# A two-layer tower on one Trainium2 core: the first layer's experts multiplied in split float32r instead of float32

## The reference, cut to what matters

```python
def _L0_ffn_ref(x, gate_w, w_gate, w_up, w_down, sh_gate, sh_up, sh_down, se_gate_w):   # 8 experts, hidden 256
    scores = xf @ gate_w.T
    ew, ei = jax.lax.top_k(scores, TOP_K)                       # 2 of 8 for each token
    ew = jax.nn.softmax(ew, axis=-1)
    x1 = jax.nn.silu(jnp.einsum('td,ehd->teh', xf, w_gate))
    x3 = jnp.einsum('td,ehd->teh', xf, w_up)
    expert_out = jnp.einsum('teh,edh->ted', x1 * x3, w_down)
    ...
    shared = jax.nn.silu(xf @ sh_gate.T) * (xf @ sh_up.T) @ sh_down.T      # hidden 512
    sgate = jax.nn.sigmoid(xf @ se_gate_w.T)
    return (routed + sgate * shared).reshape(Bb, Tt, Cc)
```

## Time and profile before

| | |
|---|---|
| median of 3 runs | 1573.73 us (1570.84 to 1576.62) |
| the profiled execution's own time | 1577.39 us |
| its span, first to last instruction | 1575.6 us |
| mean granted TensorE clock | 0.968 of full speed |
| busy: TensorE, VectorE, ScalarE, GpSimd | 1390.4, 838.1, 373.3, 480.1 us |
| moved by DMA | 197.16 MB, 125 GB/s over the span |

### The profile page before, as it was taken

How to read it: one execution, slowest core, us unless ns; L and a number is a source line. 1 busy time by engine, 2 the same in 40 slices (tenths; PEclk the granted TensorE clock), 3 DMA queues, 4 the chain that set the end, 5 groups by cost and what they waited for, 6 DMA issues and landing times.

```text
span 1575.6 us, 21975 instructions
## 1 busy us (share of the span) xinstructions
PE 1390.4 (88%) x6461; PEld 1080.0 (69%) x6462; DVE 838.1 (53%) x1729; ACT 373.3 (24%) x711; POOL 480.1 (30%) x350
## 2 busy tenths in 40 slices
PE   0595648999999999379999889999999999999997
PEld 0583316888544444237777578888888889999896
DVE  8875597755322222563667775555555543333332
ACT  1113113111111111242222312232333212222221
POOL 0661430252244443100111015632332203343332
PEclk9999779999999999798999999999999999999999
DMA  4493005201865554700000403656666579776443
GB/s 97 89 161 39 0 21 179 104 21 63 304 149 93 87 89 72 204 22 0 1 0 1 182 21 97 206 199 212 208 221 225 189 267 361 243 198 185 78 73 41
DMA packets 88931, 197.16 MB, mean 125 GB/s; under 512 B 28657, under 2 KB 32753, under 8 KB 85361
## 3 DMA queue, kind: packets, MB, share of 16 engines
q1 hardware_dynamic: 68768, 154.33, 30.1%
q0 software_dynamic: 20096, 42.02, 14.6%
HBM read 112.24 MB, written 81.02 MB: 123 GB/s over the span
## 4 chain that ended last, share of the span: by engine, by line
PE 79%; DVE 13%; issue 3%; DMA 2%; ACT 1%; POOLq 1%; POOL 0%; SPq 0%; DVEq 0%; ACTq 0%
PE ps L1533 25%; PE ps L1593 19%; PE ps L1655 9%; PE ps L2055 6%; PE ps L1681 4%; PE ps L429 4%; PE ps L1623 2%; DVE held L482 2%; PE ps L538 2%; PE ps L1669 1%; PE ps L778 1%; PE ps L2080 1%; PE ps L779 1%; PE ps L2027 1%; PE ps L2111 1%
## 5 line engine op out<-in xcount | busy, mean ns | idle before, releaser
L1593 PE MATMUL ps<-moe_rounded 128*128 128x384 f32 (+2 forms) x1800 | 374.7, 350 | 0.0
L1593 PEld LDWEIGHTS ps<-moe_rounded 128*128 128x128 f32 x1800 | 326.3, 188 | 33.3
L1300 DVE SCALAR_TENSOR_TENSOR held<-ps,moe_scratch,held 128x512 f32<-128x512 f32 (+1 forms) x255 | 187.5, 747 | 180.8 <-PE ps L1533 180.0
L1533 PE MATMUL ps<-moe_expert_parts,moe_rows_parts 128*128 (+1 forms) x1320 | 258.4, 349 | 2.5 <-DVE moe_rows_parts L1324 1.5
L1533 PE MATMUL ps<-moe_rounded 128*128 128x512 f32 (+3 forms) x885 | 242.2, 394 | 11.8 <-DVE moe_rounded L1282 9.7
L1533 PEld LDWEIGHTS ps<-moe_expert_parts,moe_rows_parts 128*128 128x128 f32 (+1 forms) x1320 | 219.6, 190 | 15.8 <-issue 3.3
L1533 PEld LDWEIGHTS ps<-moe_rounded 128*128 128x128 f32 (+2 forms) x885 | 146.7, 171 | 50.7 <-DVE moe_rounded L1282 12.0
L1310 DVE TENSOR_TENSOR moe_scratch<-moe_scratch,ps 128x256 f32<-128x256 f32 (+1 forms) x80 | 37.7, 471 | 237.2 <-ACT moe_scratch L1515 237.2
L1655 PE MATMUL ps<-moe_experts,moe_scratch 128*128 x320 | 144.2, 593 | 0.6 <-issue 0.6
L1404 POOL TENSOR_TENSOR moe_split_parts<-moe_scratch,moe_split_parts 128x704 fp32r<-128x704 f32 (+2 forms) x48 | 88.6, 1851 | 172.9 <-ACT moe_split_parts L1497 172.9
L1388 POOL DMA_INDIRECT slot_tokens<-moe_scratch x68 | 73.5, 1081 | 174.2 <-DVE held L1300 167.4
(11 more groups left out here) (311 smaller groups left out, 1686.2 us busy)
## 6 DMA issues: line engine op xcount, KB each, us to landing
moe_expert_parts<-expert_parts SPq DMA_DIRECT2D x8, 3840.0 KB, 13.0
expert_parts<-moe_split_parts SPq DMA_DIRECT2D x32, 704.0 KB
moe_scratch<-in_ffn_gate_up SPq DMA_DIRECT2D x32, 352.0 KB, 4.7
xn_rows<-moe_xn SPq DMA_DIRECT2D x2, 4096.0 KB, 12.9
moe_experts<-in_ffn_gate_up SPq DMA_DIRECT2D x8, 1024.0 KB, 6.3
expert_parts<-moe_split_parts SPq DMA_DIRECT2D x8, 1024.0 KB
moe_scratch<-in_ffn_sh_gate_up SPq DMA_DIRECT2D x15, 512.0 KB, 3.5
tokens<-sb SPq DMA_DIRECT2D x16, 256.0 KB
```

The lines of the kernel that those rows point to most:

```text
L1300: v.scalar_tensor_tensor(out=hb[0:rows, t, :], in0=ps[0:rows, ADDED[t % 3], :], scalar=sg[0:rows, t:t + 1], in1=hb[0:rows, t, :], op0=ALU. ...
L1533: mm = t.matmul(out, lhs(k, x), rhs(k, y), start=(k == 0 and i == 0), stop=(k == ks - 1 and i == 2))
L1593: mm = t.matmul(unit_banks(u, m)[j], weights(k, x, j), xT[y][:, k, unit_cols(m)], start=(k == 0 and i == 0), stop=(k == KD - 1 and i == 2))
```

## The change

Layer 0's experts now work as layer 1's: weights in two rounded parts, a ring of four slots, three matmuls for each product, hi and lo parts of the turned rows and hidden rows, and `tile_slots` in the routing. Their weights come as 48 pieces of 128x512 (six for each of the eight experts: four of gate and up, two of down), through a ring of four small slots: SP loads a piece (256 KB), ScalarE rounds it (`round`), GpSimd subtracts (`rest`), SP stores both parts (512 KB) in DRAM. Pieces 0 to 23 are made in the scan layer: four loads are put into the tokenizer's SP program, 4 roundings stand ahead of the scan layer's ScalarE program and 20 after its sigmoids; GpSimd's first four stand ahead of its additions of beta and 20 behind them. Pieces 24 to 47 are made in layer 0's shared blocks 0 to 2, eight in each. All four shared blocks of layer 0 are now written out without a loop.

The core of the diff:

```diff
+EARLY_SLOTS, EARLY_W, EARLY_CHUNKS = 4, D, KD + 2
+EARLY, EARLY_FIRST, EARLY_FRONT, EARLY_BLOCKS = NE * EARLY_CHUNKS, 4, 24, 3
+EARLY_EACH = (EARLY - EARLY_FRONT) // EARLY_BLOCKS
+class EarlyParts:
...
+    def keep(self, sp, n):
...
+        sp.wait_ge(self.lo, n + 1)
+        sp.dma_start(to, self.part(n).bitcast(F32)).then_inc(self.stored[n % EARLY_SLOTS], 16)
+    def keep_front(self, sp):
+        for n in range(EARLY_FRONT):
+            self.keep(sp, n)
+            if n + EARLY_SLOTS < EARLY_FRONT + 2:
+                self.load(sp, n + EARLY_SLOTS)
+    def round(self, s, n):
+        x, turns = n % EARLY_SLOTS, n // EARLY_SLOTS
+        s.wait_ge(self.loaded[x], 16 * (turns + 1))
+        if turns:
+            s.wait_ge(self.stored[x], 16 * turns)
+        s.activation(self.part(n)[:, 0], self.raw(n), ACT.Copy).then_inc(self.hi, 1)
+    def rest(self, p, n):
+        p.wait_ge(self.hi, n + 1)
+        p.tensor_tensor(self.part(n)[:, 1], self.raw(n), self.part(n)[:, 0], ALU.subtract).then_inc(self.lo, 1)
...
@@ sync of a mixture, layer 0
-            for e in range(2):
-                load_expert(sp, e, e_in[0])
-            more(2)
-            with sp.Fori(3, NSH) as b:
-                more(b)
+            for n in range(EARLY_FRONT + 2, EARLY_FRONT + EARLY_SLOTS):
+                early_parts.load(sp, n)
+            for b in range(EARLY_BLOCKS):
+                early_parts.keep_beside(sp, b)
+                if b + 2 < NSH:
+                    more(b + 2)
+            early_parts.all_kept(sp)
             slots_in()
-            sp.wait_ge(e_in[0], 2 * 16 * WD)
-            sp.sem_inc(rt, 1)
+        load_parts(sp, 0)
+        sp.wait_ge(e_in[0], E0 + LOADED)
+        sp.sem_inc(rt, 1)
...
@@ ScalarE, the "part" steps of a shared block
+                    if not by_block:
+                        if b < EARLY_BLOCKS:
+                            n = EARLY_FRONT + b * EARLY_EACH
+                            for k in EARLY_AT[m]:
+                                early_parts.round(s, n + k)
...
@@ GpSimd, layer 0
             for n in range(2 * T):
                 beside_adds(n)
+                for k in rest[:n % 2]:
+                    early_parts.rest(p, k)
+                rest = rest[n % 2:]
...
@@ TensorE, gate and up of a tile
-            elif 2 * F <= QC:
-                for k in range(KD):
-                    mm = t.matmul(ps[:, u, 0:2 * F], xgT[:, u, k], exg(e, k, 0, 2 * F), start=(k == 0), stop=(k == KD - 1))
+            if 2 * F <= QC:
+                mm = split_products(ps[:, u, 0:2 * F], lambda k, x: xgT[:, u, x, k],
+                                    lambda k, y: slots_w[:, slot, y * GW + k * KW:y * GW + (k + 1) * KW], KD)
...
-        ROUTING = {("lo", 0): segments, ("lo", 1): slots_of, ("lo", 2): tile_slots if split_w else tile_experts}
+        ROUTING = {("lo", 0): segments, ("lo", 1): slots_of, ("lo", 2): tile_slots}
...
+EARLY_AT = ((0, 1), (2,), (3, 4), (5,), (6,), (7,))
```

More of the change, by code:

```diff
@@ L696, in gpsimd @@
     def gpsimd(p):
+        for n in range(EARLY_FIRST):
+            early_parts.rest(p, n)
         p.wait_ge(w_fb, 16 * 7)
@@ L702, in gpsimd @@
             p.tensor_tensor(hb[0:r, n, :], hb[0:r, n, :], bet[0:r], ALU.add).then_inc(hbr, 1)
+        for n in range(EARLY_FIRST, EARLY_FRONT):
+            early_parts.rest(p, n)
         p.wait_ge(hbr, T)
@@ L709, in scalar @@
     def scalar(s):
+        for n in range(EARLY_FIRST):
+            early_parts.round(s, n)
         for k, tiles in enumerate(GROUPS):
@@ L819, in ffn_layer @@
     GW, DW = KD * 2 * F, NF * D
-    EW = 2 * (GW + DW) if split_w else GW + DW
+    EW = 2 * (GW + DW)
     SGW = KD * 2 * SF
-    if not split_w:
-        ex = g.experts[:, 0:NE * EW].rearrange("p (e w) -> p e w", e=NE)
-    exg, exd = (lambda e, k, j, w: ex[:, e, k * 2 * F + j:k * 2 * F + j + w]), (lambda e, f, r: ex[0:r, e, GW + f * D:GW + (f + 1) * D])
+    by_block = early_parts is None
     r = Arena(g.rounded, g.y_at, g.y_at)
@@ L1063, in blocks @@
     def blocks(eng, body):
-        first = FIRST if split_w else 1
+        first = FIRST if by_block else NSH - 1
         pairs = (NSH - 1 - first) // 2
@@ L1068, in blocks @@
             body(b, b % 2)
-        with eng.Fori(0, pairs) as i:
-            for k in range(2):
-                body(2 * i + first + k, (first + k) % 2)
+        if pairs:
+            with eng.Fori(0, pairs) as i:
+                for k in range(2):
+                    body(2 * i + first + k, (first + k) % 2)
         for b in range(2 * pairs + first, NSH):
@@ L1273, in block @@
             for what, m in DVE_STEPS:
-                if split_w and is_last(b) and (what, m) == ("lo", NU - 1):
+                if is_last(b) and (what, m) == ("lo", NU - 1):
                     rows_lo(0, 0)
@@ L1380, in gpsimd @@
     def gpsimd(p):
+        if not by_block:
+            for n in range(EARLY_FRONT, EARLY_FRONT + EARLY_EACH):
+                early_parts.rest(p, n)
         p.wait_ge(rt, ROUTED)
@@ L1408, in gpsimd @@
         else:
+            rest = list(range(EARLY_FRONT + EARLY_EACH, EARLY))
             for n in range(2 * T):
                 beside_adds(n)
+                for k in rest[:n % 2]:
+                    early_parts.rest(p, k)
+                rest = rest[n % 2:]
+            assert not rest
         p.wait_ge(xs, 4 * 16)
@@ L2187, in look_through @@
         self.rounded = over("moe_rounded", self.y_at, self.high_at, F32R)
-        self.experts = over("moe_experts", self.xn_at, self.xn_at + EXPERTS)
         self.expert_parts = over("moe_expert_parts", self.xn_at, self.xn_at + PARTS, F32R)
```

245 lines of the change are left out of this document (130 added, 115 removed).

## The result

The changed kernel took 1599.37 us in the median of 4 runs (1598.41 to 1600.32), the one before 1575.15 us beside it (4 runs). The ratio is 1.0158, 95% interval 1.0143 to 1.0173: 24 us slower, where 16 faster was forecast. The span of the profiled execution is 1596.6 us, against 1575.6.

What follows compares the result with a forecast made beforehand. TensorE was taken as the bound, except VectorE in block 0. The terms -28.2 + 4.8 + 5.8 + 0.7 + 0.5 = -16.4 took the profiled 1577.4 to 1561.0, or 1557 us against the runs' median; range 1545 to 1569.

Steps and rivals of the forecast that it cites:

- The expert tiles: Layer 0's expert stage: tiles fall to 4.90 us, products of 512 columns at 0.230 or 0.241; 207.0 against 235.2, -28.2 us.
- 11.0 around the tiles: Layer 1's expert stage time beyond its forty tiles, 11.0 us, charged to layer 0's new stage in place of its 2.8.
- the chain of rows: Expert tile: rows turned, copied by ScalarE, rests by VectorE; 1.95 us within 2.06, hidden. Rival if not: 1573 us, chance 0.14.
- The scan layer: Pieces made in GpSimd's and ScalarE's idle time, ring done about 213, before 220.19; +0.5 us allowed, bounds 0 and 1.6.
- By GpSimd alone: Scan layer: twenty rests of 1.52 us are 30.4, so GpSimd would end them at 206.5; the ring is slower.
- the lock: Rival in block 0: GpSimd's rests block VectorE through the shared SBUF port pair, 12.2 us, 1569.5; chance 0.04.
- Block 0: Layer 0's first shared block, set by VectorE: +4.8 us for `tile_slots`, +5.8 for a rounding ahead of unit 1's silu.
- the wait for piece 26: Block 0: the silu of unit 1 stands behind this piece's load and rounding, 5.7 us late; +5.8, bounds 0 to 6.4.
- Blocks 1 to 3: Layer 0's later shared blocks, bound by TensorE: +0.2 us each for pieces, +0.7 with block 3 unrolled and new code.
- The long tile: Rival in layer 0's expert stage: tile longer than 4.9 us; at 5.3 it costs 16 us, 1573; chance 0.14.
- The late ring: Rival in the scan layer: mixed stores and loads at 300 GB/s cost 3 us, at 260 9.5 (1567); chance 0.07.
- the slow DMA: Rival in the scan layer: the ring moves only 184 GB/s, 68.5 us, +29.5, 1587 us; chance 0.03.

Runs made afterwards that it cites:

- the first experiment: Layer 0's expert tiles 1 to 38 written out without a loop on TensorE alone, against the changed kernel: 1586.84 us, 12.5 less.

## Why the prediction was wrong

**The expert tiles: the step that failed most, 21.4 us.** I took the tile as a sum of TensorE's instructions and set 11.0 around the tiles "since the code of the loop is now the same". The code is, but what covers it is not: with a shorter tile the sequencer's own work on loads and loop registers comes to light, 13.3 us by the first experiment. The sign was in rows already seen: layer 1's stage has 11.0 around its tiles, layer 0's 2.8, and I charged it without asking what it was; I had named only the chain of rows as what could hold a tile up, and that was hidden. The other 8 us are 10.0 for 40 written-out tiles of 5.15 instead of 4.90, less 1.9 around them, and those 10.0 are for the most part the sequencer too: with the loads behind the turn a tile takes 4.94 where it is undisturbed, its 12 products 2.84 (574.49 to 577.33), so 0.237 each where I had 0.230. With tiles written out and loads behind the turn together the median tile is 5.02 and the stage 209.8, 2.8 over the forecast (1.5 of its gain is the clock, which is full there at the second tile, where the 12 products from 435.46 on take 4.44 us at 0.62 in the changed kernel). So the price of the products was nearly right. What failed is that I put the register loads and the loop at nothing beyond layer 1's 11.0.

**The scan layer: 5.8 us missed.** "By GpSimd alone" I saw free time and asked only whether the ring ends in time. It does. What it does to VectorE beside it I priced at nothing. I had the lock as a rival, but in block 0 alone and with a chance of 0.04. A sign of it was in the rows that I used. The 1.52 us for an operation of 128x512 on GpSimd is no price of one: it is the mean of 15 additions of 1.25 and the one of 5.48 beside the scan. The rests take 1.25 where nothing holds them up. The Trainium skill (SBUF - State Buffer, two separate sides) says that the one which starts first has the port pair for its whole instruction. The trace agrees at 131.28, where VectorE's 0.17 us became 1.23 behind a rest that had started at 131.23. It does not at 172.07: one addition was under way there, but the next one and three rests, which all start after the scan, run at their usual 1.25, and the scan takes 10.02. Which of the two gets through is not fixed by the order of the program either: before the change and in the run with own semaphores it was the scan, in the changed kernel the additions and rests. What decides it is open.

**Block 0: 10.6 forecast, 14.5 measured.** Here the steps held: `tile_slots` 5.6 for 4.8, the wait for piece 26 5.6 for 5.8. But 2.4 of the first 5.6 are TensorE's lower clock behind its idle time, which I never named; the 4.8 had some of it by luck, as layer 1's block 0 has such an idle time too (4.34 us, then 5.21 us for the same products). Missing was the third, 3.3 us for the pieces beside a block that VectorE sets. That layer 1's blocks with parts lose 0.2 us had told nothing of it; TensorE sets those.

**Blocks 1 to 3: 0.7 forecast, 3.4 measured.** Block 1 is 1.0 us longer than before, block 2 0.8, and block 3 with what follows it up to the first tile 1.6. Of the last, 1.4 us are the clock: the last 12 down products take 4.44 us (425.49 to 429.93) at a granted clock of 0.62 behind an idle time of 1.98 us, where they took 3.05 at 1.00 behind one of 1.78. In blocks 1 and 2 the clock is full, and TensorE waits here and there for VectorE's lo parts. The pieces in the block are not the whole of it, as block 1 with twelve of them and none in block 0 took 34.5 us; no run takes this further apart.

**Layer 1: 0 forecast, 3.7 measured.** Its lo semaphores became shared ones, counted from 40 on (`LO0 + n` in its waits). I put that at nothing.

**The rivals.** The long tile was one of them, up to 5.45 us, with the chain of rows as its cause. A long tile came, 5.63 us over a turn of the loop, through another cause. The late ring and the slow DMA did not come: of the ring's 20 rests the last was 5 us later than forecast, and still in time. A miscount changes nothing: 27 of the 40 slices of the earlier trace rows lie above 330, not 28.

## What to carry to other kernels

When matmuls leave a loop, count what its sequencer does in each turn (register loads, waits on reckoned values, the branch), as the work that covered it leaves too; a stage with microseconds "around its tiles" shows that it is near. Where the order of such loads is free, try both places: 14 us of layer 0's stage were had by moving one line, and 6 lost in layer 1's. Free time on GpSimd is not free for VectorE: look at what VectorE does beside it, above all where VectorE sets the end, and put such work beside stages that TensorE sets. Before a mean of a group is used as a price, look at its single members: one that is four times as long is a collision that the kernel already has. And where TensorE will wait some microseconds longer than before, price what follows at the lower clock too.

## What the runs showed that was not expected

- GpSimd subtractions of 128x512 (1.25 us each) stretched VectorE instructions with two SBUF inputs from 0.17 to 1.2 us, and, with an addition, a scan of 5.1 to 10.0. In the same place of another run the scan took 5.11 and the addition 5.45 instead of 1.25.
- Sharing a semaphore between two loops with an offset of 40 costs the second loop's branch tile 0.8 us (8.03 against 7.19).
- Two kernels of the same products, tiles and waits differ by 16.5 us, 14.4 of them in layer 0's expert stage, through the place of three register loads in TensorE's program.
- Behind idle times of 4.3 to 6.3 us TensorE's granted clock was at its lower level for some microseconds: the products that end block 0 took 5.2 to 6.0 us instead of 3.7.
